# Folding W^T G2^T into the Strassen groups of Y, and opening a fused cross-attention kernel with X G1^T on four batches at once

## The chip, the cores and the metric

The kernel runs on one core of one Trainium2 chip. The metric is device time in microseconds, the median of three runs. Everything is float32 data; the matrix engine (TensorE, PE) is fed "fp32r" operands, and each product of two float32 blocks is made of three matmuls: high times high, high times low and low times high, where high is the rounded copy of a block (made by ScalarE, ACT) and low is the block minus its high part (made by VectorE, DVE). SyncE (SP) issues nearly all DMAs, in program order, and waits on semaphores between them.

## The reference

For each of 16 batches, with x of 256 x 1024 and context c of 256 x 512:

```python
memory_proj = einsum('bme,de->bmd', memory, W_mem)             # c W^T
scores = einsum('bnd,bmd->bnm', hidden, memory_proj) / sqrt(D)
attn = softmax(scores)
memory_context = einsum('bnm,bmd->bnd', attn, memory_proj)
gate = sigmoid(einsum('bnf,df->bnd', concat([hidden, memory_context]), W_gate) + b_gate)
fused = hidden + gate * memory_context
out = fused * rsqrt(mean(fused**2) + EPS) * norm_w
```

The kernel regroups this. Y = X W gives the scores as Y c^T; T = attn c gives the context as T W^T and its part of the gate as T K with K = W^T G2^T; G1 and G2 are the halves of W_gate, and Z = X G1^T + bias is the rest of the gate.

## The kernel before, in words

PE's work stands in four stages, written out by hand as loops, and each engine has its own copy of the loop nest with semaphore waits.

1. **The fold**: K, 512 x 1024, as a plain product over 8 slices k of W and G2. Each slice is 4 row blocks x 2 halves x 3 = 24 matmuls of 128x512, 192 in all. `fold_high` (ACT) and `fold_low_part` (DVE) split each slice as it lands. K is copied out of PSUM (`k_out`) and stored to DRAM (`k_spill`).
2. **X G1^T**: for each batch a Strassen-like scheme of 7 products of 12 matmuls of 128x512 (`gx_mm` counts products, `gx_z` the additions into z). The 7 blocks of G1 and of its sums are made once, during the fold (`g1_cut`, `g1_t1` and so on); the blocks of x are cut one by one four products ahead (`x_cut`). z goes to DRAM. Beside it, one per batch in batches 0 to 12, the 12 weight blocks of the last stage are made: six of W^T and six of K (`load_wp`, `wp_sums`, `wp_cut`, `store_wp`), loaded to one set of buffers, summed, split and stored again. `load_wp` of a block waits until both stores of the block before have landed (`wp_stored`).
3. **Y = X W**: four groups of four batches, 7 products of 24 matmuls each (two halves `et` of 12). ACT copies four of the seven out of PSUM (`y_copy`), DVE adds three (`y_add`, two instructions each). Products share PSUM banks: PE starts product 6, sixth in the order 0, 1, 2, 3, 4, 6, 5, half by half only when DVE has added the matching half of product 4 (`y_added`). SP loads the next group's four x blocks (8 DMAs of 512 KB) at the head of a group and stores y by quarters (`store_y`).
4. **The batches**: scores, softmax, T, and the Strassen products with the blocks of W^T and K (`mem_gate`), then the gate, the norm and the output.

Within an engine all is in program order. In a Y group the DVE order at position q of the group is: `y_add` of that product, sums for the next group, `y_cut` of the product three ahead.

## Time and profile before

| | |
|---|---|
| median of 3 runs | 921.67 us (921.26 to 922.32) |
| the profiled execution, its own time | 921.56 us |
| its span, first to last instruction | 919.8 us |
| PE busy | 910.1 us, 99% |
| DVE busy | 738.1 us, 80% |
| ACT busy | 415.3 us, 45% |
| mean DMA rate over the span | 204 GB/s |
| matmuls and weight loads | 4400 each |

The span is read against the engines' busy times; the 1.8 us between the span and the execution's own time lie outside all engines. Where PE is busy nearly throughout, what counts is the number of its matmuls and each pause between them.

### The profile page before, as it was taken

The numbers are of one execution on the slowest core, as the hardware profiler recorded it, in microseconds if no ns is written. First come the engines' busy times: TensorE is split into PE (matmuls) and PEld (weight loads), VectorE is DVE, ScalarE is ACT, GpSimd is POOL, SyncE is SP. The second block draws the span as 40 slices with busy tenths as digits, with TensorE's granted clock in tenths as the row PEclk, the third lists the DMA queues.
The fourth block names the chain that finished last, engine by engine and source line by source line (L and its number), as shares of the span: only waits on it lengthen the run. The fifth ranks groups of instructions, "written<-read, shape, count | busy, mean of one in ns | idle before, by whom it ended". The sixth has DMA issues, their size and how long they took to land.

```text
span 919.8 us, 11716 instructions
## 1 busy us (share of the span) xinstructions
PE 910.1 (99%) x4400; PEld 768.0 (83%) x4400; DVE 738.1 (80%) x972; ACT 415.3 (45%) x625; POOL 54.4 (6%) x73
## 2 busy tenths in 40 slices
PE   9999999999999999999999999999999999999996
PEld 7888888888888888888888888888888888888885
DVE  5996677766777679888686689888888988888887
ACT  5442222322223224644544455556555565555553
POOL 0000000000000000000000011110111111111002
PEclk9999999999999999999999999999999999999999
DMA  8535567465674745765649924455555545445552
GB/s 339 195 130 169 198 225 253 165 222 192 209 267 168 253 168 197 266 234 196 226 155 372 364 102 170 174 206 206 207 204 185 189 164 179 176 167 179 207 183 91
DMA packets 50568, 187.41 MB, mean 204 GB/s; under 512 B 5200, under 2 KB 7248, under 8 KB 43472
## 3 DMA queue, kind: packets, MB, share of 16 engines
q1 hardware_dynamic: 50224, 186.14, 56.8%
q8 instruction: 35, 0.57, 0.2%
q10 hardware_dynamic: 288, 0.52, 0.2%
q14 instruction: 21, 0.17, 0.1%
HBM read 130.02 MB, written 56.62 MB: 203 GB/s over the span
## 4 chain that ended last, share of the span: by engine, by line
PE 97%; DVE 1%; DMA 1%; ACT 0%; SPq 0%; POOL 0%; issue 0%; DVEq 0%
PE psum L1348 32%; PE psum L1350 32%; PE psum L1349 32%; PE psum L1433 1%; DMA g_raw<-in_g 1%; ACT zb L780 0%; DVE xlast L1341 0%; DVE zb L1265 0%; DVE g_l L832 0%; ACT zb L775 0%; ACT g2h L554 0%; POOL stat L547 0%; SPq L303 0%; POOL stat L543 0%; DVE xlast L1271 0%
## 5 line engine op out<-in xcount | busy, mean ns | idle before, releaser
L1348 PE MATMUL psum<-g1h,xh 128*128 128x512 f32 x448 | 174.3, 389 | 0.0
L1349 PE MATMUL psum<-g_l,xh 128*128 128x512 f32 x448 | 174.3, 389 | 0.0
L1350 PE MATMUL psum<-g1h,xs_l 128*128 128x512 f32 x256 | 99.6, 389 | 0.0
L1349 PEld LDWEIGHTS psum<-g_l,xh 128*128 128x128 f32 x448 | 84.1, 188 | 17.5
L1348 PEld LDWEIGHTS psum<-g1h,xh 128*128 128x128 f32 x448 | 84.1, 188 | 17.3
L554 ACT ACTIVATE xh<-xs_raw 128x512 fp32r<-128x512 f32 x64 | 40.3, 631 | 118.3 <-PE psum L1350 118.3
L1223 DVE TENSOR_TENSOR zb<-psum,zb 128x512 f32<-128x512 f32 x112 | 76.8, 686 | 16.1 <-PE psum L1350 16.1
L1350 PE MATMUL psum<-g1h,xsum_l 128*128 128x512 f32 x192 | 74.7, 389 | 0.0
L947 DVE TENSOR_TENSOR z<-psum,bias 128x512 f32<-128x512 f32 x64 | 44.2, 690 | 35.7 <-PE psum L1350 35.7
L529 POOL TENSOR_TENSOR stat<-stat 128x1 f32<-128x1 f32 x30 | 19.8, 660 | 846.8 <-ACT zb L768 846.8
L554 ACT ACTIVATE xh<-xsum_raw 128x512 fp32r<-128x512 f32 x48 | 30.1, 629 | 79.9 <-PE psum L1350 75.7
L947 DVE TENSOR_TENSOR z<-psum,z 128x512 f32<-128x512 f32 x48 | 33.2, 691 | 36.1 <-PE psum L1350 36.1
L1350 PEld LDWEIGHTS psum<-g1h,xs_l 128*128 128x128 f32 x256 | 48.0, 188 | 10.0
L763 ACT ACTIVATE zb<-zb 128x1024 f32<-128x1024 f32 x30 | 31.7, 1055 | 50.8 <-DVE zb L1223 50.8
L768 ACT ACTIVATE zb<-xrow 128x1024 f32<-128x1024 f32 x30 | 31.9, 1062 | 43.7 <-DVE xrow L1237 43.7
L1348 PE MATMUL psum<-yh,ws_h 128*128 128x512 f32 x128 | 50.0, 391 | 0.0
L1350 PE MATMUL psum<-yh,ws_l 128*128 128x512 f32 x128 | 49.8, 389 | 0.0
L832 DVE TENSOR_TENSOR xs_l<-xs_raw,xh 128x512 fp32r<-128x512 f32 x64 | 43.9, 687 | 1.9 <-ACT xh L554 1.7
L832 DVE TENSOR_TENSOR t_l<-t_full,th 128x256 fp32r<-128x256 f32 x48 | 20.2, 421 | 30.7 <-ACT th L554 30.7
L1350 PEld LDWEIGHTS psum<-g1h,xsum_l 128*128 128x128 f32 x192 | 36.0, 188 | 7.5
L554 ACT ACTIVATE y<-psum 128x512 f32<-128x512 f32 x32 | 18.6, 599 | 49.3 <-PE psum L1350 29.9
L1248 DVE SCALAR_TENSOR_TENSOR xrow<-xrow,stat,norm 128x1024 f32<-128x1024 f32 x30 | 38.3, 1278 | 0.1
(177 smaller groups left out, 2421.1 us busy)
## 6 DMA issues: line engine op xcount, KB each, us to landing
xs_raw<-in_xt SPq DMA_DIRECT2D x16, 1024.0 KB, 4.8
z_spill<-z SPq DMA_DIRECT2D x16, 1024.0 KB, 7.7
b_raw<-in_xt SPq DMA_DIRECT2D x32, 512.0 KB, 7.5
zb<-z_spill SPq DMA_DIRECT2D x16, 1024.0 KB, 6.7
xrow<-in_x SPq DMA_DIRECT2D x30, 512.0 KB, 6.5
out<-xrow SPq DMA_DIRECT2D x30, 512.0 KB, 3.7
y_spill<-y SPq DMA_DIRECT2D x32, 256.0 KB, 3.0
yt_raw<-y_spill SPq DMA_DIRECT2D x16, 512.0 KB, 3.7
```

The costliest lines, as they stand in the source:

```text
L529: pool.tensor_tensor(guarded[:, nb:nb + 1], meansq[:, nb:nb + 1], eps, ALU.add).then_inc(guarded_done, 1)
L554: return nc.scalar.activation(dst, src, ACT.Copy)
L763: nc.scalar.activation(zb[b % 2][:, nb, :], zb[b % 2][:, nb, :], ACT.Tanh, scale=0.5).then_inc(tanh_done, 1)
L768: nc.scalar.activation(zb[b % 2][:, nb, :], xrow[:, nb, :], ACT.Square, scale=SCALE, accum_out=meansq[:, nb:nb + 1]).then_inc(sq_done, 1)
L832: return nc.vector.tensor_tensor(dst, src, high.bitcast(F32), ALU.subtract)
L947: nc.vector.tensor_tensor(dst, bank(bk), more, ALU.add).then_inc(gx_z, 1)
L1223: nc.vector.tensor_tensor(dst, bank(bk), dst, ALU.add).then_inc(z_done, 1)
L1248: nc.vector.scalar_tensor_tensor(xrow[:, nb, :], xrow[:, nb, :], rstd[:, nb:nb + 1], norm[:, :], ALU.mult, ALU.mult).then_inc(row_done, 1)
L1348: nc.tensor.matmul(tile, ah, mh, start=start, stop=False, skip_group_check=True)
L1349: nc.tensor.matmul(tile, ah, ml, start=False, stop=False, skip_group_check=True)
L1350: return nc.tensor.matmul(tile, al, mh, start=False, stop=stop, skip_group_check=True)
L1433: last = nc.tensor.transpose(psum[:, 5, N * mb + PART * nb:N * mb + PART * nb + PART], prob[:, nb, PART * mb:PART * mb + PART], ident[:, :])
```

## The change: what it does

The fold is gone. K is computed as a fifth group of Y, which stands first: the group of Y with s = 0 takes its "x" blocks from G2^T (`g2t`, laid out like xt) and its result rows in the y store are K. Groups 1 to 4 are the old 0 to 3. The program then opens with X G1^T of the first four batches side by side: for each of the seven products one stage of 4 x 12 matmuls, all four batches with the same block of G1. Stage order is `R_ORDER = [0, 1, 3, 2, 5, 4, 6]`. Stage 0 loads its operands by slices of k; the sums of G1 and of x for a stage are made on DVE just ahead of it. Batches 4 to 15 follow as before.

The blocks of W^T for the last stage are made beside batches 6 to 11; the blocks of K, which exists only after the first Y group, are made in Y groups 1, 2 and 3, at positions 3 and 6 of each (`K_AT`). Their order is 1, T2, T4, B22, T3, T1. The low parts of 1, T2 and T1 are written by DVE to their final place and not stored (`wp_direct`). W's quadrants, formerly left over from the fold, are loaded and split beside batches 5 and 12 to 14 (`w_cut`).

```diff
-            for k in range(1, KD):
-                pe.wait_ge(fold_low, 2 * k + 1)
-                slot = G2_SLOT[k]
-                for e in range(KE):
-                    wh, wl = w_part(wn_high, k, e, 0), w_part(wn_low, k, e, 1)
-                    for h in range(2):
-                        last = three(bank(fold_bank(e, h)), wh, wl, g2_h[slot][:, HALF[h]], g2_l[slot][:, HALF[h]],
-                                     False, k == KD - 1)
+            for stage in range(2, P7):
+                i = R_ORDER[stage]
+                pe.wait_ge(g1_low, G1_CUT[i])
+                for j in range(NR):
+                    pe.wait_ge(x_low, NR * (stage - 2) + j + 1)
+                    pe.wait_ge(gx_z, NR * {3: 1, 2: 0, 5: 2, 4: 3, 6: 5}[i] + j + 1)
+                    for k in range(4):
+                        last = three(bank(r_bank(j, i)), xh[j][:, k, :], R_LOW[i][:, k, j, :], g1_h[i][:, k, :],
+                                     g1_l[i][:, k, :], k == 0 and i == 3, k == 3)
+                    last.then_inc(gx_mm, 1)
...
+            for stage in range(2, P7):
+                i = R_ORDER[stage]
+                if i in (S1, S2):
+                    g1_sums((T1, T2)[i == S2])
+                elif i == S4:
+                    g1_sums(T3)
+                if i != 6:
+                    r_sums(i)
+                g1_cut(i)
+                for j in range(NR):
+                    r_cut(stage, j)
+                    r_out(stage - 1, j)
+                if i == S4:
+                    g1_sums(T4)
...
             for k in range(4):
-                load_fold(k)
-            load_g1(0)
-            load_g1(T3)
+                load_first(k)
+            for h in range(2):
+                ks = slice(2 * h, 2 * h + 2)
+                sp.dma_start(r_a12[:, ks, :, :], xr[1][:, ks, :, :]).then_inc(r12_in[h], DMA)
+                sp.dma_start(g1_raw[T4][:, ks, :], g1[2][:, ks, :]).then_inc(g1_b21_in[h], DMA)
             sp.dma_start(bias[:, :], b_gate.rearrange("(a d) -> a d", a=1).to_broadcast((PART, D))
                          ).then_inc(bias_in, DMA)
+            sp.dma_start(g1_raw[T3][:, :, :], g1[1]).then_inc(g1_b12_in, DMA)
+            sp.dma_start(r_a21[:, :, :, :], xr[2]).then_inc(r21_in, DMA)
+            sp.dma_start(r_a22[:, :, :, :], xr[3]).then_inc(r22_in, DMA)
+            sp.dma_start(g1_raw[B22][:, :, :], g1[3]).then_inc(g1_b22_in, DMA)
...
+        K_AT = {(s, q): N_WT + n for n, (s, q) in enumerate((s, q) for s in (1, 2, 3) for q in (3, 6))}
...
                 sp.wait_ge(y_mm, 2 * P7 * s + 4)
                 load_x_block(s + 1, 1, 0)
+                if s == 1:
+                    sp.wait_ge(ws_sum, 4)
+                    sp.wait_ge(ws_low, WS_CUT[S1])
+                elif s >= 2:
+                    store_wp(K_AT[s - 1, 6])
+                if s >= 1:
+                    load_wp(K_AT[s, 3])
                 store_y(s, 0)
...
+                if s >= 1:
+                    store_wp(K_AT[s, 3])
+                    load_wp(K_AT[s, 6])
                 store_y(s, 2)
                 store_y(s, 3)
...
                     if i == 5:
                         y_add(s, i)
+                    if (s, q) in K_AT:
+                        for j in range(WP_SUMS[wp_blocks[K_AT[s, q]][1]]):
+                            wp_sums(K_AT[s, q], j)
                     if n < Y_LAST - YH and q != 3:
                         y_cut(n + YH)
-                    if s in (1, 2) and q == 2:
-                        wb0_cut(s - 1)
+                    if (s, q) in K_AT:
+                        wp_cut(K_AT[s, q])
```

DVE in the opening of the changed program, from just after stage 0's outputs to the first cut of stage 2. `g_2_raw` is the sum T1 of G1, `r_s_raw` the sum S1 of the four batches' x, `zr` their outputs, and `r_l_l` the low part that stage 2 multiplies:

```order
L979 TENSOR_TENSOR g_2_raw<-g_4_raw,b_came 128x2048 [waits g1_b12_in]
L1002 TENSOR_TENSOR r_s_raw<-r_a_raw 128x2048 [waits r22_in,r21_in]
L944 TENSOR_TENSOR g_3_l<-g_2_raw,g1h_55 128x2048 [waits g1_high]
L944 TENSOR_TENSOR r_l_l<-r_s_raw,xh_101 128x4x128 [waits gx_mm,x_high]
L1043 TENSOR_TENSOR zr_0_122<-psum,zr_0_122 128x512 [waits gx_z,gx_mm]
L944 TENSOR_TENSOR r_l_l<-r_s_raw,xh_102 128x4x128 [waits gx_mm,x_high]
```

This is new: before, DVE made such sums of G1 between slices of the fold, and no x was summed for four batches at once.

DVE in the middle of a Y group, before (the third group). The row `y_160<-psum` is the addition of product 1, the row `y_159<-psum` that of product 4:

```order
L1044 TENSOR_TENSOR y_160<-psum,y_160 128x2x256 [waits y_copied,y_mm] x2
L832 TENSOR_TENSOR b_0_l<-b_0_raw,yh_155 128x2048 [waits y_high]
L832 TENSOR_TENSOR yt_l<-yt_raw,yh_156 128x2048 [waits y_high]
L832 TENSOR_TENSOR wb_0l<-wb_raw,wb_0h 128x1024 [waits wb0_high]
L1044 TENSOR_TENSOR y_159<-psum,y_159 128x2x256 [waits y_copied,y_mm] x2
```

And now, in the group of the changed program with s = 2:

```order
L1216 TENSOR_TENSOR y_194<-psum,y_194 128x2x256 [waits y_copied,y_mm] x2
L944 TENSOR_TENSOR b_2_l<-b_2_raw,yh_190 128x2048 [waits y_high]
L944 TENSOR_TENSOR yt_l<-yt_raw,yh_191 128x2048 [waits y_high]
L1139 TENSOR_TENSOR wp_raw<-wp_raw,wp_other 128x1024 [waits wp_in]
L944 TENSOR_TENSOR wp_l<-wp_raw,wp_h 128x1024 [waits wp_high]
L1216 TENSOR_TENSOR y_193<-psum,y_193 128x2x256 [waits y_copied,y_mm] x2
```

Two rows of a K block, one of them waiting for a load (`wp_in`), stand ahead of the addition of product 4. The group with s = 3 reads the same; that with s = 1 has the cut alone.

SP in the same stretch, before (loads of the next group's x, then the store of a quarter of y):

```order
L350 DMA b_raw<-in_xt 128x1024 [waits y_mm]
L350 DMA b_raw<-in_xt 128x1024
L412 DMA y_spill<-y_159 128x512 [waits y_added]
L412 DMA y_spill<-y_159 128x512
L401 DMA wb_1l<-wb_low_spill 128x1024 [waits ws_sum]
```

And now, at s = 3:

```order
L402 DMA b_raw<-in_xt 128x1024 [waits y_mm]
L402 DMA b_raw<-in_xt 128x1024
L424 DMA wb_high_spill<-wp_h 128x1024 [waits wp_low]
L426 DMA wb_low_spill<-wp_l 128x1024
L418 DMA wp_raw<-y_spill 128x2x256 [waits y1_stored,wp_stored]
L418 DMA wp_raw<-y_spill 128x2x256
L418 DMA wp_other<-y_spill 128x2x256 [waits y0_stored]
L418 DMA wp_other<-y_spill 128x2x256
L478 DMA y_spill<-y_195 128x512 [waits y_added]
```

The last block's store, a wait until it has landed, and the next block's load stand between the loads of x and the store of y. At s = 2 there is one store and two loads; at s = 1 no store and two loads.

## Rows read from the trace of the kernel before

**Rows 1.** The page's first part, and the clock of the core.

```profile
PE 910.1 (99%) x4400; PEld 768.0 (83%) x4400; DVE 738.1 (80%) x972; ACT 415.3 (45%) x625; POOL 54.4 (6%) x73
...
core 0: 919.8 us, clock 0.998
```

**Rows 2.** Who PE waited for, whole span: total, times, longest.

```profile
PE psum L1359 <- POOL stat L521: 1.0, 1, 1.0
PE psum L1376 <- DVE g2h L837: 0.3, 1, 0.3
```

**Rows 3.** Timeline of PE in the fold: start, duration, instruction.

```profile
10.96 0.50 PE L1348 MATMUL psum<-g2h,wn_h 128*128 128x512 f32 x1
...
11.76 0.40 PE L1348 MATMUL psum<-g2h,wn_h 128*128 128x512 f32 x1
...
25.37 0.39 PE L1348 MATMUL psum<-g2h,wn_h 128*128 128x512 f32 x1
```

**Rows 4.** Timeline of the opening; in brackets the idle time before.

```profile
4.80 2.42 PE L1376 MATMUL psum<-g2h,wn_h 128*128 128x512 f32 x8 [0.31 <-DVE g2h L837]
...
7.31 0.63 ACT L554 ACTIVATE wn_h<-wn_raw 128x512 fp32r<-128x512 f32 x1 [1.33 <-DMA wn_raw<-in_wn]
```

**Rows 5.** ACT starts that a landing DMA released, the windows of 12 to 16 and 21 to 22 us.

```profile
15.23 1.92 ACT L554 ACTIVATE g1h<-g_raw 128x2048 fp32r<-128x2048 f32 x1 [1.43 <-DMA g_raw<-in_g]
...
25.77 1.06 ACT L554 ACTIVATE g2h<-g_raw 128x1024 fp32r<-128x1024 f32 x1 [0.64 <-DMA g_raw<-in_g]
...
12.00:16.00 4.00, 4.00 (x19) 3.33 (x18) 2.88 (x3) 2.15 (x3) 0.00 (x0) 1.00 1.01 421
...
q8 instruction: 1, 0.02, 6.8%
```

**Rows 6.** Timeline of DVE in the opening, four instructions back to back.

```profile
20.02 2.29 DVE L832 TENSOR_TENSOR g_l<-g_raw,g1h 128x2048 fp32r<-128x2048 f32 x1
22.22 0.69 DVE L832 TENSOR_TENSOR wn_l<-wn_raw,wn_h 128x512 fp32r<-128x512 f32 x1
22.82 1.22 DVE L832 TENSOR_TENSOR g_l<-g_raw,g2h 128x1024 fp32r<-128x1024 f32 x1
23.96 2.29 DVE L870 TENSOR_TENSOR g_raw<-g_raw,g_raw 128x2048 f32<-128x2048 f32 x1
```

**Rows 7.** Timeline of SP in the third Y group.

```profile
435.86 6.12 SPq L350 DMA_DIRECT2D b_raw<-in_xt  x8
444.71 0.80 SPq L412 DMA_DIRECT2D y_spill<-y  x2
```

**Rows 8.** Landing times: b_raw from 430 to 445 us (min/median/max), y_spill of 444 to 446 us.

```profile
DMA to landing us min/median/max: 5.6/8.1/9.7
...
y_spill<-y SPq DMA_DIRECT2D x2, 256.0 KB, 6.8
```

**Rows 9.** DMA issues of 60 to 340 us by tile: count, KB each, us to landing.

```profile
wp_raw<-in_wt SPq DMA_DIRECT2D x6, 512.0 KB, 4.2
...
wp_other<-in_wt SPq DMA_DIRECT2D x3, 512.0 KB, 5.7
```

**Rows 10.** Timeline of DVE, ACT and PE in the third Y group (PE from 430.1 us).

```profile
451.27 1.22 DVE L832 TENSOR_TENSOR wb_0l<-wb_raw,wb_0h 128x1024 fp32r<-128x1024 f32 x1
454.79 0.69 DVE L1044 TENSOR_TENSOR y<-psum,y 128x512 f32<-128x512 f32 x1 [2.30 <-PE psum L1350]
...
471.75 1.28 DVE L1044 TENSOR_TENSOR y<-psum,y 128x512 f32<-128x512 f32 x2
...
452.56 1.91 ACT L554 ACTIVATE yh<-b_raw 128x2048 fp32r<-128x2048 f32 x1
...
457.31 0.39 PE L1348 MATMUL psum<-yh,wn_h 128*128 128x512 f32 x1
```

**Rows 11.** Timeline of ACT in the third Y group, a split of 128x1024.

```profile
443.01 1.04 ACT L554 ACTIVATE wb_0h<-wb_raw 128x1024 fp32r<-128x1024 f32 x1
```

More of the change, by code:

```diff
@@ L99, in build @@
+        b22_raw, b22_l = zip(*[raw_low(f"b22_{s}", [PART, 2, 4, N], (1, 193)[s % 2]) for s in range(SB)])
         t1_raw, t1_l = raw_low("yt1", [PART, 2, 4, N], 17)
@@ L364, in store_wp @@
                 sp.wait_ge(wp_low, n + 1)
-                sp.dma_start(wbhd[m, i], wp_h[:, :, :].bitcast(F32)).then_inc(wp_stored, DMA)
-                sp.dma_start(wbld[m, i], wp_l[:, :, :].bitcast(F32)).then_inc(wp_stored, DMA)
-            for b in range(B):
+                sp.dma_start(wbhd[m, i], wp_h[m][:, :, :].bitcast(F32)).then_inc(wp_stored, DMA)
+                if not wp_direct(n):
+                    sp.dma_start(wbld[m, i], wp_l[m][:, :, :].bitcast(F32)).then_inc(wp_stored, DMA)
+            for b in range(NR, B):
                 if b < B - 1:
@@ new lines, in r_cut_high @@
+            def r_cut_high(stage, j):
+                i = R_ORDER[stage]
+                if i == 6:
+                    act.wait_ge(r22_in, DMA)
+                else:
+                    act.wait_ge(r_sum, R_SUM[i])
+                if stage > 2:
+                    act.wait_ge(gx_mm, NR * (stage - 1) + j + 1)
+                elif j < 2:
+                    act.wait_ge(r_slice, 2)
+                else:
+                    act.wait_ge(gx_mm, 2 * NR)
+                copy(xh[j][:, :, :], R_RAW[i][:, :, j, :]).then_inc(x_high, 1)
@@ L580, in ws_cut_high, with w_cut_high @@
+            def w_cut_high(q):
+                act.wait_ge(w_in[q], DMA)
+                copy(w_h[q][:, :, :], w_rl[q][0][:, :, :]).then_inc(w_high, 1)
             def ws_cut_high(j):
@@ new lines, in r_cut, with r_out @@
+            def r_cut(stage, j):
+                i = R_ORDER[stage]
+                dve.wait_ge(x_high, NR * (stage - 2) + j + 1)
+                if i == S1:
+                    dve.wait_ge(gx_mm, NR)
+                elif i == S2:
+                    dve.wait_ge(x_low, NR)
+                elif i == 6:
+                    dve.wait_ge(r_sum, R_SUM[S1])
+                low(R_LOW[i][:, :, j, :], R_RAW[i][:, :, j, :], xh[j][:, :, :]).then_inc(x_low, 1)
+            def r_out(stage, j):
+                i = R_ORDER[stage]
+                first, c12, c22 = (zr[c][j][:, :] for c in range(3))
+                dve.wait_ge(gx_mm, NR * stage + j + 1)
+                if stage == 0:
+                    dve.wait_ge(bias_in, DMA)
+                elif i == 6:
+                    dve.wait_ge(zr_first, DMA * NR)
+                dst, more = {0: (first, bias[:, HALF[0]]), 1: (first, None), 3: (c22, bias[:, HALF[1]]),
+                             2: (c12, bias[:, HALF[1]]), 5: (c12, None), 4: (c22, None), 6: (first, bias[:, HALF[0]])}[i]
+                if more is None:
+                    dve.wait_ge(gx_z, NR * {1: 0, 5: 3, 4: 2}[i] + j + 1)
+                    more = dst
+                nc.vector.tensor_tensor(dst, bank(r_bank(j, i)), more, ALU.add).then_inc(gx_z, 1)
@@ L1394, in _ @@
+            for n in range(X_FIRST, GX_LAST):
                 b, i = n // P7, n % P7
```

636 lines of the change are left out of this document (351 added, 285 removed).

## The prediction

> **What bounds the kernel now.** I read the page's busy times first: PE is busy 99% of the span, and the core's clock is 0.998 of full, the 2.4 GHz level throughout [rows 1]. Then who PE waited for: 1.3 us in all, at the start [rows 2]. So there is no stage where another engine is late; the time is the count of PE's matmuls plus its pauses. Then the pace: from 11.76 to 25.37 us, 60 matmuls of 128x512 are issued, 0.2268 us each [rows 3]; the 389 ns durations overlap and are not the price. The last question, which the busy shares cannot answer, is how much slack each hand-over to PE has where the change touches it: the timeline of DVE, ACT and SP in the opening and in a Y group.
>
> The sum is made against the profiled execution, 921.56 us, of which 919.8 are the span. The median is 921.67, 0.11 more, and I add that at the end. About 0.2%, or 1.8 us, is what a measurement of this kernel can tell from no change.
>
> **Term 1, the matmuls removed.** The fold has 192, the fifth Y group 7 x 2 x 12 = 168. The 28 products of batches 0 to 3 are the same, only in another order. 24 x 0.2268 = **-5.4 us**.
>
> **Term 2, the opening.** Before, 24 matmuls are done by 10.96 us and from there PE never pauses [rows 3]. Its operands came easily: 24 matmuls needed 768 KB. Now a stage of 48 matmuls (10.9 us) needs up to 3 MB, and DVE must form sums over four batches.
> - Start: as before, the first matmul at 4.80 [rows 4]; the first 12 end by 7.7. Slice 1's second operand has the place in the queue of the W slice whose landing ACT used at 7.31 [rows 4]; ACT 0.63 and DVE 0.69 [rows 6] give 8.7. A pause of 1.0, but stage 2 is late whatever stage 0 does.
> - Stage 2 waits for S1, a sum over the third and fourth quarters of x. Counted in issue order, these are complete after 7.86 MB. Before, exactly 7.86 MB were queued up to the G2 slice that released ACT at 25.77, and 4.19 MB up to 15.23 [rows 5]. At the 421 GB/s of 12 to 16 us the other 3.67 MB would take 8.7 us and land at 23.9; one packet of PE's instructions at 21 to 22 us took 6.8% of 16 engines for 1 us, 1.1 us of one engine [rows 5], and the queue behind it lands later. PE will have issued nearly as many instructions then, so I keep that packet. I take A = 25.0; the ends are 25.8 (same bytes, same time) and 23.6 (when DVE is free: it cuts the second operands after stage 0 ends at 16.8, adds four outputs, then forms T1).
> - From A, DVE does two instructions of 2048 at a pace of 2.20 (20.02 to 22.22), one of 512 at 0.60 (22.22 to 22.82) and one output of 0.69 [rows 6]: 2.20 + 2.20 + 0.60 + 0.69 = 5.7. Stage 2 starts at 30.7, while stages 0 and 1 end at 16.8 + 10.9 = 27.7: PE stands 3.0 us.
> - At 30.7 the kernel before has done 24 + (30.7 - 10.96) / 0.2268 = 111 matmuls, the new one 96. The 15 matmuls are 3.4 us.
> - Later stages: DVE needs 3 x 2.20 + 8 x 0.60 = 11.4 per stage against PE's 10.9, and 2.2 more for T4. Followed through in order, stage 3 starts without a pause, stage 4 is 0.4 late, stage 5 0.5, and stage 6 has slack. Together 0.9.
>
> Term 2 is **+4.3** (2.9 to 5.1 over the ends of A). Terms 1 and 2 together are -1.1, from -2.5 to -0.3.
>
> **Term 3, the K blocks in the Y groups.** Times are those of the third group before, where PE starts at 430.1; product 6 follows product 4 at 457.31 [rows 10]. It needs DVE's addition of product 4's first half. That was done at 454.79 + 0.69 = 455.5, slack 1.8 us. Now a K block stands ahead of it on DVE, in program order (the order rows above), behind a chain across SP:
> - SP issues eight x loads of 512 KB from 435.86 on, the last at about 441.6 [rows 7]; the slowest took 9.7 us to land, at 451.3, and y_spill, issued at 444.71, landed 6.8 later, at 451.5, against a size of only 512 KB in two [rows 7, 8]. The queue is served in order, so a store issued at 442 is behind 4 MB.
> - s = 1: no store, loads only. ACT's split of the block comes after its yh split, 452.56 + 1.91 = 454.5, plus 1.04 [rows 10, 11], then DVE 1.22 for the cut and 0.69: 457.4, 0.1 late.
> - s = 2 (T4): one store, 512 KB, lands at 451.5. Only then SP issues the load. 512 KB take 4.2 [rows 9]: 455.7. Sum 1.22, split 1.04, cut 1.22, addition 0.69 [rows 10, 11]: 459.9, so 2.6 us late.
> - s = 3 (T3): two stores, 1 MB, land 1.3 later (512 KB at 421 GB/s [rows 5]), at 452.8; two sources, 1 MB, 5.5 after the first issue (between the 4.2 of a first and the 5.7 of a second load [rows 9], issued 0.9 later): 458.3. The same four instructions: 462.5, 5.2 late. The group starts with DVE about 0.5 earlier after the pause in s = 2, so 4.7.
>
> Together **+7.4**. Lower end: stores land at 450.5 and loads in 3.0: 0.4 and 1.9, so 2.4. Upper end: 1 us more on each chain, and 1 us at the head of group 2, where DVE is already 3.6 us behind PE at a group's end (471.75 [rows 10] against 430.1 + 168 x 0.2268 = 468.2) and two sums of T2 are put behind that addition. I count that place at nothing: by the same steps the next addition of product 1 ends about 0.6 before PE needs it.
>
> **Costed at nothing.** K's copy and store to DRAM, its blocks' splits beside batches 0 to 12, and W's split: ACT is 45% busy and PE waited for none of it [rows 1, 2]. The last group's loads of finished blocks are now behind the last store, some 5 us later, but the first is needed only 40 us later. If that cover went, `mem_gate` would wait at its second product.
>
> The sum: -5.4 + 4.3 + 7.4 = +6.3; 921.56 + 6.3 = 927.9, and with 0.11 for the median 928.0.
>
> **The clock rule.** The clock fell nowhere before, but no pause of PE was over 1.0 us [rows 1, 2], so no row prices a long one. Two pauses here would be 3.0 and 4.7 us. The Trainium skill (TensorE: Matmul & The Clock Gate, section "HAM oscillation") says that an array left idle long enough returns to half clock and then works slowly until activity releases it; by that rule the sum would be that of rival 2, 931.6, not 928.0. No row shows it, so my sum has zero.
>
> **Rivals.**
> 1. *The loads come in time* (the other side). The addition of product 4 decides from the point where a K block's load lands by 457.3 - 0.69 - 1.22 - 1.04 - 1.22 = 453.1. If stores overtake the queued x loads, or SP's wait ends early, term 3 is near 0.1 and terms 1 and 2 remain: 920.7, or 919.3 with A at its early end, where PE's 24 fewer matmuls show most. For it: DMA engines are idle in parts of the group, and y_spill's own 6.8 us is hardly more than x's share before it. Against: landings grow from 5.6 to 9.7 us in order of issue [rows 8]. Chance 0.18, about half of it beyond the 0.2%.
> 2. *The clock falls* after the two long pauses. At 1.2 GHz each 128x512 matmul costs 0.2268 more; one product of 24 would be 5.4. I take 8 matmuls per pause, an estimate between none and a product: 2 x 1.8 = 3.6 more, 931.6. Chance 0.17.
> 3. *The change does less than it says*: that the opening does not pause, because S1's operands land by 20 us. Excluded in effect by 7.86 MB at 421 GB/s; no chance of its own.
>
> **How the numbers follow.** The forecast case, both kinds of pause at full clock, has 0.65; its own range is 923.0 to 931.0, from the ends of terms 2 and 3. The predicted time is that case's, 928.0. The range reaches down to rival 1's edge and up to rival 2: 921.0 to 932.0. Faster 0.09, within 0.2% 0.12, slower 0.79.
>
> **What would show it.** In the new trace: 24 fewer matmuls; the x quarters r_a21 and r_a22 landing near 25 us; a PE pause of about 3 us near 28 and small ones before stages 4 and 5; in the second, third and fourth Y group a pause of 0.1, 2.6 and 4.7 us before product 6, with PE waiting for the DVE addition of y, DVE waiting for ACT's wp_h or for the load of wp_raw, and SP waiting for wb_high_spill. After each pause the clock row must read full. The prediction is wrong if PE has no pause in those groups, or if SP's wait for the store ends before 449 on that time scale.

## The result, and the profile after

The changed kernel takes **932.67 us** (median of 4 runs, 930.95 to 936.77) against 921.71 us (921.26 to 922.32, 4 runs) on the same chip: a ratio of 1.0125, 95% interval 1.0091 to 1.0159. It is slower by 11.0 us, where 6.3 were forecast; the range ended at 932.0, 0.7 below the median. The profiled execution took 932.3 us, of which 930.6 are the span, 10.8 more than the span of before.

The page's first part and the clock of the core, as in [rows 1]:

```profile
PE 910.1 (98%) x4376; PEld 765.6 (82%) x4376; DVE 751.0 (81%) x961; ACT 420.6 (45%) x624; POOL 54.4 (6%) x73
```

```profile
core 0: 930.6 us, clock 0.995
```

PE has 24 matmuls fewer, and yet the same 910.1 us of busy time: some matmuls got longer, and the clock's mean fell from 0.998. Who PE waited for over the span (two rows of 0.3 and 0.2 us left out):

```profile
PE psum L1524 <- DVE y L1216: 7.2, 2, 4.4
PE psum L1524 <- DVE zr L1043: 3.2, 1, 3.2
PE psum L1531 <- POOL stat L606: 1.0, 1, 1.0
PE psum L1542 <- DVE g1h L949: 0.3, 1, 0.3
```

In [rows 2] it was 1.3 us in all. L1216 is `y_add` in the Y groups, L1043 `r_out` in the opening. PE's timeline in the group with s = 3, at the border of product 4 and product 6:

```profile
461.36 0.39 PE L1525 MATMUL psum<-b_l,ws_h 128*128 128x512 f32 x1
461.58 0.39 PE L1526 MATMUL psum<-yh,ws_l 128*128 128x512 f32 x1
466.35 0.47 PE L1524 MATMUL psum<-yh,w_h 128*128 128x512 f32 x1 [4.38 <-DVE y L1216]
466.65 0.59 PE L1525 MATMUL psum<-yt_l,w_h 128*128 128x512 f32 x1
467.04 0.63 PE L1526 MATMUL psum<-yh,w_l 128*128 128x512 f32 x1
467.47 0.63 PE L1524 MATMUL psum<-yh,w_h 128*128 128x512 f32 x1
```

From the start at 461.58 to the one at 466.35 it is 4.77 us, so 4.54 beyond the pace of 0.2268. And then the starts lie 0.43 us apart, for 8 matmuls. The granted clock says what that is. Windows of the same trace (length, then busy us and count of PE, PEld, DVE, ACT and POOL, then the granted clock, the DMA share and GB/s):

```profile
422.00:426.00 4.00, 4.00 (x11) 3.14 (x12) 4.00 (x3) 0.00 (x0) 0.00 (x0) 0.57 0.70 272
426.00:430.00 4.00, 4.00 (x19) 3.29 (x18) 4.00 (x3) 1.23 (x3) 0.00 (x0) 1.00 0.42 107
466.00:470.00 4.00, 3.65 (x9) 2.91 (x10) 4.00 (x4) 0.14 (x1) 0.00 (x0) 0.59 0.65 262
31.00:35.00 4.00, 3.55 (x16) 2.95 (x17) 4.00 (x8) 0.00 (x0) 0.00 (x0) 1.00 0.46 174
```

After both Y pauses (2.98 us behind the matmul that starts at 418.79, 4.54 behind that at 461.58) the clock stood at the 1.2 GHz level for most of 4 us: 11 and 9 matmuls in windows where 17 to 19 fit. After the opening's pause of 3.3 us it did not, in this execution.

What held `y_add` was a chain on DVE; ACT's split of the sum (from 463.29, 1.06 us) lies between its first two rows:

```profile
461.97 1.23 DVE L1139 TENSOR_TENSOR wp_raw<-wp_raw,wp_other 128x1024 f32<-128x1024 f32 x1 [6.11 <-DMA wp_other<-y_spill]
464.38 1.23 DVE L944 TENSOR_TENSOR wp_l<-wp_raw,wp_h 128x1024 fp32r<-128x1024 f32 x1 [1.18 <-ACT wp_h L639]
465.52 1.28 DVE L1216 TENSOR_TENSOR y<-psum,y 128x512 f32<-128x512 f32 x2
```

And what held that load shows in SP's timeline, to be read against [rows 7]:

```profile
438.18 8.30 SPq L402 DMA_DIRECT2D b_raw<-in_xt  x8
447.00 0.43 SPq L426 DMA_DIRECT2D wb_low_spill<-wp_l  x1
455.12 0.88 SPq L418 DMA_DIRECT2D wp_raw<-y_spill  x2
456.05 0.98 SPq L418 DMA_DIRECT2D wp_other<-y_spill  x2
```

SP's waits for the stores over 385 to 520 us (total, times, longest):

```profile
SPq L418 <- DMA wb_low_spill<-wp_l: 15.6, 3, 7.6
SPq L418 <- DMA wb_high_spill<-wp_h: 9.2, 1, 9.2
```

Between the store at 447.00 and the load at 455.12 SP does nothing but wait.

In the opening, this is DVE's timeline at the border of stages 1 and 2:

```profile
25.61 2.29 DVE L1002 TENSOR_TENSOR r_s_raw<-r_a_raw 128x2048 f32<-128x2048 f32 x1 [1.19 <-DMA r_a_raw<-in_xr]
27.82 2.28 DVE L944 TENSOR_TENSOR g_l<-g_raw,g1h 128x2048 fp32r<-128x2048 f32 x1
30.02 0.69 DVE L944 TENSOR_TENSOR r_l_l<-r_s_raw,xh 128x512 fp32r<-128x512 f32 x1
30.62 0.68 DVE L1043 TENSOR_TENSOR zr<-psum,zr 128x512 f32<-128x512 f32 x1
```

And PE's:

```profile
27.91 0.39 PE L1526 MATMUL psum<-g1h,r_l_l 128*128 128x512 f32 x1
31.45 0.47 PE L1524 MATMUL psum<-g1h,xh 128*128 128x512 f32 x1 [3.16 <-DVE zr L1043]
```

**The ledger** is made from the starts of PE's matmuls in both traces. It counts, in us, everything beyond the pace:

| | forecast | measured |
|---|---|---|
| 24 matmuls fewer | -5.4 | -5.4 |
| start of the first matmul (4.80 to 5.11) | 0 | +0.3 |
| first slices of stage 0, against the same place of before | +0.4 | +0.4 |
| before stage 2 / before stages 4 and 5 | +3.0 / +0.9 | +3.4 / +0.9 |
| Y groups s = 1, 2, 3 | +0.1, +2.6, +4.7 | +0.2, +3.0, +4.6 |
| matmuls at 1.2 GHz, 8 after each Y pause | 0 | +3.1 |
| sum | +6.3 | +10.5, of 10.8 |

The measured pauses include the longer first step behind each (0.08). The forecast's 3.4 for stages 0 to 2 is split here by its own steps. Of the 4.2 us between the two sums 3.1 are the clock.

### The profile page after: what moved, and what is told of

It is laid out like the page before. It is cut to its first block, busy times and chain, and to the rows that moved or that the text cites. A ratio compares the mean times of both kernels' runs of the same rounds, so it can differ in the third digit from the quotient of the medians.

```text
span 930.6 us, 11736 instructions
## 1 busy us (share of the span) xinstructions
PE 910.1 (98%) x4376; PEld 765.6 (82%) x4376; DVE 751.0 (81%) x961; ACT 420.6 (45%) x624; POOL 54.4 (6%) x73
## 4 chain that ended last, share of the span: by engine, by line
PE 91%; DMA 5%; DVE 1%; SPq 1%; issue 1%; ACT 1%; POOL 0%; DVEq 0%; ACTq 0%
PE psum L1524 30%; PE psum L1525 30%; PE psum L1526 30%; DMA r_a_raw<-in_xr 2%; DMA wb_high_spill<-wp_h 1%; DMA wb_low_spill<-wp_l 1%; PE psum L1623 1%; DMA wp_other<-y_spill 1%; DMA wp_raw<-y_spill 0%; DVE wp_raw L1139 0%; ACT wp_h L639 0%; SPq L418 0%; SPq L402 0%; SPq L365 0%; ACT zb L892 0%
## 5 line engine op out<-in xcount | busy, mean ns | idle before, releaser
L1524 PE MATMUL psum<-g1h,xh 128*128 128x512 f32 x416 | 162.1, 390 | 3.5 <-DVE zr L1043 3.2
L1525 PE MATMUL psum<-g_l,xh 128*128 128x512 f32 x416 | 161.9, 389 | 0.0
L1526 PE MATMUL psum<-g1h,xs_l 128*128 128x512 f32 x192 | 74.7, 389 | 0.0
L1524 PE MATMUL psum<-yh,ws_h 128*128 128x512 f32 x160 | 62.4, 390 | 0.0
L1526 PE MATMUL psum<-yh,ws_l 128*128 128x512 f32 x160 | 62.3, 389 | 0.0
L1526 PE MATMUL psum<-g1h,xsum_l 128*128 128x512 f32 x144 | 56.0, 389 | 0.0
L1524 PE MATMUL psum<-yh,w_h 128*128 128x512 f32 x120 | 48.0, 400 | 7.2 <-DVE y L1216 7.2
L1526 PE MATMUL psum<-yh,w_l 128*128 128x512 f32 x120 | 48.2, 401 | 0.0
L944 DVE TENSOR_TENSOR b_l<-b_raw,yh 128x2048 fp32r<-128x2048 f32 x20 | 45.8, 2288 | 2.4 <-ACT yh L639 1.9
L639 ACT ACTIVATE yh<-b_raw 128x2048 fp32r<-128x2048 f32 x20 | 38.3, 1914 | 15.4 <-PE psum L1526 12.5
L944 DVE TENSOR_TENSOR t_l<-t_full,th 128x256 fp32r<-128x256 f32 x48 | 20.2, 421 | 30.7 <-ACT th L639 30.7
```

The source lines that it names most:

```text
L639: return nc.scalar.activation(dst, src, ACT.Copy)
L944: return nc.vector.tensor_tensor(dst, src, high.bitcast(F32), ALU.subtract)
L1524: nc.tensor.matmul(tile, ah, mh, start=start, stop=False, skip_group_check=True)
L1525: nc.tensor.matmul(tile, ah, ml, start=False, stop=False, skip_group_check=True)
L1526: return nc.tensor.matmul(tile, al, mh, start=False, stop=stop, skip_group_check=True)
```

## The experiments

Three questions: is it the store and load chain that makes the Y pauses; does PE's rest itself bring the half clock; and what limits the opening. Times are medians; "before" was 921.65 to 921.71 in each set of runs.

**1. Make DVE's K work come later.** In groups s = 1 to 3 the K block of position 3 is summed and cut between the two halves of product 4's addition.

```diff
-                    if i in (1, 4):
+                    if i == 4 and (s, 3) in K_AT:
+                        y_add(s, i, lambda: (k_sums(s, 3), wp_cut(K_AT[s, 3])))
+                    elif i in (1, 4):
                         y_add(s, i)
```

> DVE does the K block of position 3 between the two halves of product 4's addition, not ahead of both; SP's order is untouched. Queue theory (the addition stands behind a block whose load waits for a store that lands behind the x loads): the first half is free at once, the second has 2.7 us more, so the pauses before product 6 fall from 2.98 and 4.54 us to about 0.3 and 1.8, too short for the clock to fall; time about 924. Work theory (DVE has too many instructions in these groups, the load is not the matter): the same instructions are only reordered, later ones move back, and the time stays above 929. Clock theory alone (the half-clock stretches are there whatever the pause): 2 x 1.6 us stay, about 927.

Measured: 930.91 us (930.65 to 933.08), ratio 1.0105, 1.0090 to 1.0120. At s = 2 the pause shrank from 2.98 to 0.41 us, as expected, and no slow matmuls followed. At s = 3 it was 6.26 us where 1.8 were expected: DVE's sum began at 462.74 us, released by the load of `wp_other`, against 461.97 in the changed kernel. PE got to product 6 some 3.8 us earlier (it ended the first half's 12 matmuls at 460.8, where the changed kernel would have begun it at 461.8), the load did not. So what was saved at s = 2 was given back at s = 3, with 10 slow matmuls behind that pause. The x loads ahead of the store were issued at 438.16 (438.18 in the changed kernel) although PE was earlier: they stand behind a store of y, for which SP waited 7.4 us until DVE's addition at 435.97 was done (435.99 in the changed kernel). The time is the one that the work theory gave, over 929, but DVE had stood idle for 6.53 us before its sum at 462.74: it was the load that was late, not DVE.

**2. Make SP's part come earlier.** SP stores the last K block and loads the next after four of the eight x loads.

```diff
                 load_x_block(s + 1, 1, 1)
+                if s >= 2:
+                    store_wp(K_AT[s - 1, 6])
+                    load_wp(K_AT[s, 3])
                 sp.wait_ge(y_mm, 2 * P7 * s + 2)
...
-                elif s >= 2:
-                    store_wp(K_AT[s - 1, 6])
-                if s >= 1:
                     load_wp(K_AT[s, 3])
```

> SP stores the last K block and loads the next one after four of the eight x loads of a group, not after all eight (groups 2 and 3); DVE, ACT and PE keep their order. Queue theory: store and load land before DVE asks (by about 18 and 20 us of the group, it asks at 21), both pauses before product 6 and both half-clock stretches go, 7.5 + 3.2 us less, time 921.5 to 922.5. Work theory: DVE's order and work are the same, so the pauses stay within 1 us of 2.98 and 4.54, time about 931.

Measured: 925.83 us (924.09 to 926.33), ratio 1.0041, 1.0026 to 1.0056. The queue theory had both pauses gone and 921.5 to 922.5. The pause at s = 2 is gone, that at s = 3 is still 1.45 us. SP there, and then DVE:

```profile
439.17 0.58 SPq L426 DMA_DIRECT2D wb_low_spill<-wp_l  x1
448.49 0.89 SPq L418 DMA_DIRECT2D wp_raw<-y_spill  x2
```

```profile
454.90 1.23 DVE L1139 TENSOR_TENSOR wp_raw<-wp_raw,wp_other 128x1024 f32<-128x1024 f32 x1 [3.02 <-DMA wp_other<-y_spill]
```

With 2 MB of x ahead in place of 4 the store still took 9.3 us to land. In this trace the opening's pause, 3.36 us, was followed by 8 matmuls at 0.43 us. Up to there this kernel does the same as the changed one, whose pause of 3.3 us was not. So the same pause keeps the clock in one execution and loses it in another.

**3. Keep PE busy in the pauses.** 12 and 18 spare matmuls into a free bank, before product 6 of s = 2 and s = 3.

```diff
+                if i == 6 and s in (2, 3):
+                    ...
+                    for _ in range((12, 18)[s - 2]):
+                        nc.tensor.matmul(spare, wh[:, 0, 0:PART], yh[n % YH][:, :, 0, :], start=True, stop=True,
+                                         skip_group_check=True)
```

> 12 and 18 spare matmuls of 128x512 (2.7 and 4.1 us) into a free bank ahead of product 6 in groups 2 and 3; they are extra work, in time in which PE stood. Clock theory (the array fell to 1.2 GHz because it stood): the pause in real work stays 3.0 and 4.5, but the matmuls after it are issued every 0.23 us, not 0.43; time 3 us less than the changed kernel, about 929.5, and less spread. If something else slows those matmuls (DMA or DVE traffic in that stretch), they stay at 0.43 and the time is 932 or more.

Measured: 932.08 us (931.14 to 934.95), ratio 1.0109, 1.0092 to 1.0126: no gain that can be told. At s = 2 it went as the clock theory says: all spare matmuls ran at the full pace, then came 0.45 us of rest, then the full pace again. At s = 3 the load landed at 464.7 in place of 462.0, the 18 did not reach, 3.17 us of rest were left, and 8 slow matmuls came. As a test of the clock it is one for and none against, and the place at s = 3 tests nothing. As a remedy it failed, because it treats the pause's length as given.

**4. Experiment 2, and the sums of x in the opening batch by batch**, so that stage 2 need not wait for all four.

```diff
+                if i != 6:
+                    r_sums(i, 0)
...
                 for j in range(NR):
+                    if i != 6 and j + 1 < NR:
+                        r_sums(i, j + 1)
                     r_cut(stage, j)
```

> The run e2_sp_early, with the four-batch sums of x (S1, S2, S4, S3) made batch by batch, 4 x 512 in place of 2048, only the first ahead of the cut of G1. If stage 2's start is set by the chain after the landing: its pause falls from 3.3 to 1.7 us. If the opening as a whole is bound by DVE's work per stage (11.4 us against PE's 10.9), most of it comes back as longer pauses before stages 3 to 5, and the time is only 0.5 to 1.0 below e2_sp_early. If the chain is all that matters, 1.6 below.

Measured: 927.75 us (926.5 to 929.98), ratio 1.0068, 1.0052 to 1.0084, slower than experiment 2. Expected was a gain of 0.5 to 1.6 us. The pause before stage 2 fell from 3.36 to 2.52 us, where 1.7 was expected, but those before stages 4 and 5 became 0.55 and 2.13. DVE, which had no idle time in these stages, now stood twice for ACT's split of a sum of G1, 1.38 us from 37.99 and 1.43 from 62.69: with only a quarter of x summed ahead, it comes to the cut sooner than ACT can have split. What PE gained in front it waited for behind. And 7 to 8 slow matmuls followed each of the rests of 2.52, 2.13 and 2.29 us.

**5. Take the wait out of the chain.** SP doesn't wait for the store before the load; ACT waits for it, before it overwrites the buffer that the store reads. Only T2, whose third source lies in that buffer, keeps the old wait.

```diff
-                if n >= 1:
+                if n >= 1 and not wait_on_act(n):
                     sp.wait_ge(wp_stored, DMA * wp_stores_by[n - 1])
...
+                if wait_on_act(n):
+                    act.wait_ge(wp_stored, DMA * wp_stores_by[n - 1])
                 copy(wp_h[m][:, :, :], wp_source(n)).then_inc(wp_high, 1)
```

> The changed kernel, but for five of the six K blocks SP no longer waits until the block before has landed in DRAM before it issues the next block's load; ACT waits for that landing instead, before it writes the high part into the buffer that the store read. What is computed stays. Chain theory: the pauses before product 6 are store landing plus load landing in series (9.2 + 4.6 us at s=2). With both in the queue together the load lands some 1.3 us (512 KB) to 2.5 us (1 MB) behind the store, so about 414.7 on the scale of the changed kernel's trace, where DVE's share of the work had to begin by 414.6, and 457.6 against 457.4: pauses of 0 to 0.5 at s=2 and 0 to 1.2 at s=3, no stretch with 0.43 us per matmul in the Y groups, 922 to 924.5 in all. Queue theory (the load is late because the DMA engines are full, not because SP waited): the load lands no sooner, pauses stay over 2 us, 928 or more.

Measured: 926.95 us (926.93 to 927.95), ratio 1.0060, 1.0045 to 1.0075. At s = 2 the pause is 0.26 us, as the chain theory has it. At s = 3 it is 3.09, followed by 8 slow matmuls. DVE at s = 2 and s = 3, and SP's issue of the load for the latter:

```profile
415.27 1.23 DVE L1144 TENSOR_TENSOR wp_raw<-wp_raw,wp_other 128x1024 f32<-128x1024 f32 x1 [1.84 <-DMA wp_raw<-y_spill]
...
456.55 1.23 DVE L1144 TENSOR_TENSOR wp_raw<-wp_raw,wp_other 128x1024 f32<-128x1024 f32 x1 [4.68 <-DMA wp_other<-y_spill]
```

```profile
443.50 0.94 SPq L421 DMA_DIRECT2D wp_raw<-y_spill  x2
```

The load is issued 11.6 us sooner than in the changed kernel (443.50 against 455.12) and releases DVE only 5.4 us sooner. PE, no longer held at s = 2, was itself 4.0 us earlier at that place (it could have begun product 6 at 457.8 in place of 461.8), so the pause shrank only from 4.54 to 3.09. The chain theory had 922 to 924.5, the queue theory 928 or more, and both hold a part: at s = 2 it was the wait, at s = 3 the wait and the queue, in which 4 MB of x and 1 MB of stores stand ahead.

**6. Fill the opening's pause too.** Experiment 5 with 12 matmuls whose weights are zero, before stage 2.

```diff
+                if stage == 2:
+                    ...
+                    for _ in range(12):
+                        nc.tensor.matmul(bank(r_bank(3, 0)), zeros[:, :], g1_h[1][:, 0, :], start=False, stop=False,
+                                         skip_group_check=True)
```

> The kernel of e5_wait_moved with 12 spare matmuls of 128x512 (weights all zero, added to a bank whose content they do not change) between stage 1 and stage 2 of the opening, in the 3.3 us in which PE has nothing to do. 12 x 0.2268 = 2.7 us. Clock theory: PE's rest in the opening shrinks to about 0.6 us, no matmul of stage 2 takes 0.43 us, in any execution; the median is 0 to 1.8 us under e5_wait_moved's, by how many of its executions lost the clock there, and the spread of the runs narrows. If the half-speed matmuls after a pause have nothing to do with PE's rest, 8 of them still stand in stage 2 and the time is that of e5_wait_moved.

Measured: 928.20 us (927.36 to 928.99), ratio 1.0071, 1.0056 to 1.0086. No slow matmul stands behind the filled rest, but none stood there in experiment 5's trace either, whose rest was 2.03 us. The time is 1.2 us over that kernel; in its trace the pause at s = 3 is 4.10 in place of 3.09. It says nothing on the clock: a pause elsewhere that moves by a microsecond drowns the effect.

**7. DVE's order in the opening.** Experiment 5, with the sum T1 ahead of stage 0's outputs and its cut ahead of the sum S1.

```diff
+            g1_sums(T1)
             for j in range(NR):
                 r_out(0, j)
+            g1_cut(S1)
```

> The kernel of e5_wait_moved with DVE's order in the opening changed: the sum T1 of G1 goes ahead of the four outputs of stage 0, its cut ahead of the sum S1 of x, and in stage 2 each output of stage 1 ahead of the cut. DVE stood idle 1.2 us ahead of S1 in the changed kernel, waiting for the last quarter of x. Theory that DVE's queue sets the opening: stage 2 starts 1.1 us earlier (pause 3.3 to 2.2), DVE is 1.1 ahead in all later stages, the pauses of 0.3 and 0.4 before stages 4 and 5 vanish: 1.1 to 1.8 us faster than e5_wait_moved, 1.8 more where the clock no longer falls. Rival: the landing of x alone sets it, and nothing changes.

Measured: 926.28 us (925.14 to 927.71), ratio 1.0054, 1.0037 to 1.0071. Stage 2 started at 30.28 us in place of 31.45 in the changed kernel's trace, 1.2 sooner, as expected: DVE's queue behind the landing did set it. Experiment 5's own trace (31.73) can't be compared here, for its stages 0 and 1 ended at 29.7 us, those of this trace at 27.9. The reason is a difference at the start that no edit made: in the traces of experiments 1, 5, 6 and 11 PE's first 10 or 11 steps took 0.42 us or more each, until 9.8 to 10.4 us. That is the pace of the 1.2 GHz level, though the row of the clock reads 1.00 there. The pauses before stages 4 and 5 stayed (0.33, 0.41), against the expectation. The median is 0.7 lower, within the scatter of the two.

**8. Two sums to GpSimd.** Experiment 5, with T3 and T4 of G1 made on GpSimd.

```diff
+            pool.wait_ge(g1_sum, G1_SUM[T2])
+            pool.tensor_tensor(g1_raw[T3][:, :, :], g1_raw[B22][:, :, :], g1_raw[T3][:, :, :], ALU.subtract
+                               ).then_inc(g1_sum, 1)
```

> The kernel of e5_wait_moved with the sums T3 and T4 of G1 (two instructions of 128x2048, 2.2 us each on DVE) made on GpSimd. Theory that DVE's queue is over PE's pace in stages 2 to 5 (11.4 us against 10.9): DVE is 2.2 us ahead before stage 4, the pauses of 0.3 and 0.4 us go, 0.5 to 0.8 us faster; the pause of 3.3 us before stage 2 stays. Rival: GpSimd's work slows DVE's instructions beside it, whose durations rise over 2.29 us, and the time is equal or longer.

Measured: 932.45 us (931.78 to 932.82), ratio 1.0116, 1.0101 to 1.0131: 5.5 us slower. GpSimd's timeline, and DVE's, in stage 3:

```profile
36.79 9.41 POOL L615 TENSOR_TENSOR g_raw<-g_raw,g_raw 128x2048 f32<-128x2048 f32 x1 [35.37 <-DVE t_made L995]
```

```profile
42.24 4.52 DVE L955 TENSOR_TENSOR r_s_l<-r_l_raw,xh 128x512 fp32r<-128x512 f32 x1
46.68 0.68 DVE L1054 TENSOR_TENSOR zr<-psum,bias 128x512 f32<-128x512 f32 x1
47.28 4.46 DVE L955 TENSOR_TENSOR r_s_l<-r_l_raw,xh 128x512 fp32r<-128x512 f32 x1
```

Two DVE cuts of 0.68 us took 4.5 us each: 7.6 us lost to save 4.4. The rival held. PE stood 4.0 us for it, in three pauses (0.63, 2.11 and 1.24). DVE wasn't slowed evenly, it was held up whole, in instructions that read two tensors from SBUF, while the output between them, with one operand in PSUM, took its usual 0.68. GpSimd's first sum, beside which DVE ran on up to 42.2, took 9.41 us, the second, of the same size, 5.02. The Trainium skill (SBUF — State Buffer, section "SBUF: two separate sides") describes the port pair that VectorE and GpSimd share as a lock: the loser blocks until the other's instruction is done. By that rule this trace agrees.

**9. Experiments 2 and 5 together**: 2 MB fewer ahead of the load, and no wait.

> The changes of e2_sp_early and e5_wait_moved together: SP stores the last K block and issues the load of the next after four of the eight x loads, and does not wait for the store before the load. Before it, only 2 MB of x are queued in place of 4 MB. Queue theory for s=3 (6 MB stand in the queue up to the end of T3's load, and the load lands with the last byte): 2 MB less are 5 us less at some 400 GB/s, so the load that released DVE at 456.55 in e5_wait_moved lands at 451 to 452, and no pause stands before product 6 in any Y group, nor any half-speed stretch there. That is 3.1 of pause and 1.6 of slow matmuls less than e5_wait_moved: 922.0 to 923.0. If instead the x loads, now later, hold up DVE's or ACT's cuts of the next group, a new pause stands before product 0 or 1 of a group.

Measured: **922.28 us** (921.62 to 924.26, 11 runs), ratio 1.0008, 0.9999 to 1.0017. Who PE waited for, and a window of the opening:

```profile
PE psum L1529 <- DVE zr L1048: 3.3, 1, 3.3
PE psum L1536 <- POOL stat L609: 1.0, 1, 1.0
```

```profile
32.00:36.00 4.00, 4.00 (x12) 3.11 (x12) 4.00 (x6) 0.00 (x0) 0.00 (x0) 0.57 0.62 234
```

No wait for y is left in any Y group. With the edits of the two experiments together 10.4 of the 11.0 us are gone, as expected (922.0 to 923.0), while DVE and ACT still make every K block at its place. So the Y groups' loss was the chain of store, load and queue, with the clock's share behind it. The window shows what remains: in this trace its pause of 3.42 us was followed by slow matmuls.

**10. The price of a rest by itself.** The kernel before the change, with nine rests of PE in Y groups, each while GpSimd writes a scratch tile a number of times.

```diff
+            for rest, (g, q, n) in enumerate(RESTS):
+                pool.wait_ge(y_mm, 2 * (P7 * g + q))
+                for m in range(n):
+                    pool.wait_ge(rest_done, sum(RESTS_N[:rest]) + m)
+                    pool.memset(scratch[:, :], 1.0).then_inc(rest_done, 1)
...
+                for rest, (g, at_q, _) in enumerate(RESTS):
+                    if (s, q) == (g, at_q):
+                        pe.wait_ge(rest_done, sum(RESTS_N[:rest + 1]))
```

> The kernel BEFORE the change, with nine rests of PE of different lengths put between products of the first three Y groups: PE waits until GpSimd, started by the end of the product before, has written a scratch tile 6 to 28 times. Nothing else is added. It prices the rests and what follows them by themselves. Clock theory: after the short ones (under 2 us) the matmuls keep 0.2268 us; after long ones (over 3 us) 6 to 13 matmuls take 0.43 us, 0.2 more each, so each long rest costs its own length and 1.3 to 2.5 us more; in between both are seen. If the slow stretches of the changed kernel came from DMA or DVE traffic in those places and not from the rest, all nine are followed by the full pace.

Measured: 978.61 us (977.37 to 979.65), ratio 1.0622, 1.0605 to 1.0639. Two of the rests on PE's timeline, of 2.00 and of 2.63 us, and the windows behind them and behind the one of 3.94 us (columns as above):

```profile
399.62 0.39 PE L1361 MATMUL psum<-yh,wn_l 128*128 128x512 f32 x1
401.85 0.47 PE L1359 MATMUL psum<-yh,ws_h 128*128 128x512 f32 x1 [1.84 <-POOL scratch L535]
402.15 0.40 PE L1360 MATMUL psum<-b_l,ws_h 128*128 128x512 f32 x1
402.39 0.39 PE L1361 MATMUL psum<-yh,ws_l 128*128 128x512 f32 x1
...
435.72 0.39 PE L1361 MATMUL psum<-yh,ws_l 128*128 128x512 f32 x1
438.58 0.77 PE L1359 MATMUL psum<-yh,ws_h 128*128 128x512 f32 x1 [2.47 <-issue]
439.14 0.63 PE L1360 MATMUL psum<-b_l,ws_h 128*128 128x512 f32 x1
```

```profile
402.00:406.00 4.00, 4.00 (x18) 3.30 (x19) 3.87 (x3) 0.45 (x1) 0.00 (x0) 1.00 0.25 91
438.60:441.80 3.20, 3.20 (x8) 2.55 (x9) 0.00 (x0) 0.00 (x0) 0.00 (x0) 0.51 0.00 0
422.00:426.00 4.00, 3.80 (x9) 3.06 (x10) 1.01 (x1) 0.00 (x0) 0.10 (x1) 0.50 1.02 414
```

All nine, worked out from the starts in the profiled execution, in order of length (us beyond the pace; matmuls slower than the pace behind it; what these cost):

```
rest   2.00  2.63  2.89  3.57  3.94  4.73  5.67  6.57  7.62
slow      1     7     9    10    14     8     8    11     9
cost   0.07  1.53  1.68  1.69  2.84  1.68  1.60  2.25  1.88
```

The rests are 39.6 us, what follows them 15.2, together 54.8 of the 55.8 that the span grew. In the window from 438.60 the clock is at its lower level while DVE, ACT, GpSimd and the DMA engines do nothing at all; in that from 422.00 the DMA engines are busy throughout. So the half clock needs no DMA or DVE traffic, and no block of K is made in this kernel's Y groups: PE's rest alone brings it, and it costs 1.5 to 2.8 us whatever the length from 2.6 us on. The Trainium skill (TensorE: Matmul & The Clock Gate, section "HAM oscillation") has this rule, that an idle array falls back to the lower clock until activity releases it; the runs agree, and at the prices above.

**11. Experiment 9 with the DVE order of experiment 7.**

> The kernel of e9_both with the DVE order of e7_t1_early in the opening. There it started stage 2 about 1.3 us sooner in the trace (pause to 30.3 in place of 31.5) and was 0.7 us faster in the median. Theory: the same here, so 0.7 to 1.3 under e9_both, 921.0 to 922.0, which is no difference from before that can be measured; the opening's remaining pauses (2.4 + 0.3 + 0.4, and 0.8 in stage 0) eat most of the 5.4 us that the 24 removed matmuls give. Rival: without the Y pauses the time is under 920.5, so the change is a gain.

Measured: 921.87 us (920.83 to 923.88, 11 runs), ratio 1.0003, 0.9994 to 1.0012. As expected, no difference from before. The profiled execution is the slowest of the eleven (923.88 us). Its mean clock reads 0.998, but its first matmul came at 5.38 us and those of its first slice are slow:

```profile
5.38 2.07 PE L1553 MATMUL psum<-g1h,rh 128*128 128x512 f32 x4 [0.56 <-DVE g1h L954]
7.25 1.91 PE L1557 MATMUL psum<-g1h,r_l_l 128*128 128x512 f32 x4
```

They lost 2.5 us against the pace, where the changed kernel's trace lost 1.2. Stage 2 started at 31.84 us, no sooner than in experiment 5's trace: with a start as slow as in these two traces the order of experiment 7 gained nothing.

**12. Experiment 11 with 8 zero-weight matmuls in the rest before stage 2.**

> The kernel of e11_t1 with 8 spare matmuls of 128x512 (zero weights, 1.8 us) in its rest of 2.2 us before stage 2, as e6_open_fill had 12. Of e11_t1's executions those near 921 had a mean clock of 0.997, those near 921.8 and above mostly 0.995 to 0.996. Clock theory: e10_rests says that a rest of 2.6 us and more was followed by 7 to 14 slow matmuls (1.5 to 2.8 us) and one of 2.0 us was not; with the rest filled, no execution has a slow stretch, all show 0.997 or more, the median is 920.8 to 921.4, a gain of 0 to 0.1% on before, and the runs lie closer together. If the spread of e11_t1 comes from the start alone (first matmul between 5.0 and 5.5 us), clock and median stay as they are.

Measured: **920.64 us** (920.31 to 922.30, 11 runs), ratio 0.9992, 0.9983 to 1.0002. PE at that border, and the window behind it:

```profile
28.01 1.97 PE L1596 MATMUL psum<-g1h,zeros 128*128 128x512 f32 x8
30.20 0.47 PE L1538 MATMUL psum<-g1h,xh 128*128 128x512 f32 x1 [0.21 <-issue]
```

```profile
32.00:36.00 4.00, 4.00 (x20) 3.29 (x19) 4.00 (x5) 0.07 (x1) 0.00 (x0) 1.00 0.41 154
```

All eleven executions show a mean clock of 0.997 or 0.998, where experiment 11's went down to 0.995, and the median is 1.2 us lower, 0.2 under the range that was expected. The pause is as long as in experiment 11 (2.19 us), only filled with matmuls that change nothing, and by these means the clock held behind it in every execution. That the fill made the whole 1.2 us is not shown. The expectation says that experiment 11's slower executions are those with the lower mean clock, but they are not: its six at 0.997 or 0.998 have a median of 922.4, its five at 0.995 or 0.996 one of 921.7. The two kernels also ran on different chips (before has 921.71 on both), and the start, which the mean clock doesn't show, was slow in experiment 11's trace and not in this one. Against before it is 1.1 us in the medians, a gain that the interval doesn't quite separate from none.

## Why the prediction was right in direction and short in size

- **What bounds the kernel**, PE's count of matmuls and its pauses: right, but for the pace behind a pause. With that the ledger closes to 0.3 us.
- **Term 1**, -5.4: right.
- **Term 2, the opening.** The landing of the last quarter of x was forecast for 25.0 and released DVE at 25.61. Stage 2 started at 31.45, forecast 30.7, but stages 0 and 1 ended 0.4 later too, so the pause was 3.3 against 3.0; the 0.4 and 0.5 before stages 4 and 5 were 0.29 and 0.42. The step "Start: as before, the first matmul at 4.80" was 0.3 short. The term came out at +5.0 against +4.3. Across the experiments the first matmul starts between 4.96 and 5.95 us, and in four traces stages 0 and 1 ended 1.4 to 1.8 us later than in the changed kernel's, most of it for slow matmuls at the start; where nothing filled it, the pause before stage 2 was then 1.1 to 1.3 us shorter.
- **Term 3, the K blocks.** 0.2, 3.0 and 4.6 against 0.1, 2.6 and 4.7, by the mechanism that was put: SP waits for the store, the load lands, DVE sums, ACT splits, DVE cuts, and only then `y_add`. At s = 2 the landings fit too: counted from the group's start, the store landed 0.2 us after the forecast and the load 0.2. At s = 3 the close fit is in part luck: there the store landed 2.2 us sooner than forecast, because the x loads went out 2.2 sooner, and the load then took 6.9 us in place of 5.5. Experiments 2, 5 and 9 take the chain apart link by link. The queue's part in it (a load late because of the x ahead of it, not because SP waited) shows best in experiment 5.
- **The clock, the step that failed.** "No row shows it, so my sum has zero." Zero was one end of an unknown, not its middle: the trace of before had no pause over 1.0 us, so it spoke neither for a fall nor against one, and the estimate of rival 2 (8 matmuls and 1.8 us per pause) lay ready, with a chance of 0.17. What the runs showed in its place: a rest of PE by itself, from 2.6 us on, is followed by matmuls at the half clock, which cost 1.5 to 2.8 us (experiment 10). In the changed kernel it was 8 matmuls and 1.6 us after each of two pauses, 3.1 of the 4.2 us between the sums. Rival 2's 931.6 was 1.1 from the median, with some luck: its two pauses were the opening's and that at s = 3, while in the trace the clock fell at s = 2 and s = 3 and not in the opening.
- **The range.** Its upper end stood at rival 2's bare value, with none of the width that terms 2 and 3 had of themselves (up to 3.1 above the forecast, by the text's own 931.0). The two together reach 934.6, and the median lies in that. (Added up outright, the ends that the text gives for terms 2 and 3 make 921.6 to 932.8; its 923.0 to 931.0 takes them as not all at once, without saying so.)
- **Rival 1**, loads in time, came true nowhere in the changed kernel; experiment 9 is that case made by hand. It gave 922.28 where the text had 920.7. Of the difference 0.7 is the opening; the rest is probably the clock there, which fell in the profiled execution (1.5 us).
- **Costed at nothing**: nothing of it shows. No pause of PE over 0.1 us lies behind the Y groups.
- **The 4 runs' spread**, 930.95 to 936.77, is wider than any kernel's of before. Mean clocks of 0.987 to 0.995 go with it. The likely reason, which only the opening's rest shows in traces, is that the three long rests (3.3, 3.0, 4.5) lose the clock in some executions and not in others, or for longer. How the slowest, at 0.987, divides among them no trace shows.

What stays open: why a rest of 3.3 us kept the clock in one trace, while others of 2.13 to 2.52 us lost it, in experiment 4; why the first matmuls are slow until about 10 us in some executions and not in others; and whether the small gain of experiment 12 over before is real, and whether it comes from the filled rest.

## What to carry to other kernels

Where PE never rests, any pause that a change brings can have two prices: its length, and 1.3 to 2.8 us of slow matmuls behind it, which came in these traces after some rests between 2.1 and 3.4 us and after all longer ones. Put the second into the sum as soon as the first is there, and into the spread of the runs too. Where a short rest can't be avoided, a few matmuls that change nothing kept the clock here (experiment 12, and experiment 3 at s = 2).

A wait on a DMA queue that sits between two transfers costs more than its own landing: it puts the landings of a store and a load one behind the other. Move it to the engine that overwrites the buffer, and put the transfer that someone waits for ahead of the bulk loads that no one does. Neither was enough alone here (5.7 and 6.8 of 11.0 us, in this order); together they gave back 10.4.

Before shifting DVE's work to GpSimd, look at whether DVE's instructions in that stretch read two tensors from SBUF; here 14 us of GpSimd's cost DVE 7.6.

## What the runs showed of the hardware that was not expected

- The half clock came after rests as short as 2.13 us (experiment 4, before stage 5) and failed to come after 3.31 us (the changed kernel's opening) and after 2.00, 2.03, 2.05, 2.11, 2.18 and 2.35 us (experiments 10, 5, 1, 8, 11, 7). Between these lengths the length alone doesn't decide.
- How many of the first matmuls run at the slow pace differs from trace to trace: in experiment 11's the steps until 10.2 us took 0.42 us or more, in the changed kernel's no step did behind the one of 5.11. The mean clock of the execution didn't show it (0.998).
- The half clock needn't begin with the first matmul behind the rest: after the one of 3.57 us in experiment 10, matmuls from 369.03 to 370.03 us kept the full pace, and the slow ones began at 370.03.
- A store of 1 MB behind 2 MB of loads took 9.3 us to land (experiment 2), more than the 8.1 behind 4 MB in the changed kernel, whose loads had been issued over 8.3 us in place of 1.9. The bytes issued ahead didn't give the landing time; in both the store had landed 12.3 and 16.9 us after the first x load.
